# A selective-scan layer laid out as 4 states x 32 channels per tile instead of 128 channels per state

## The chip, the cores and the metric

The program runs on one core of a Trainium2 chip. The metric is the device time of one execution, in microseconds (us). Five engines work side by side, each through its own queue in program order, and meet through semaphores: TensorE (PE; its weight loads are shown as PEld), VectorE (DVE), ScalarE (ACT), GpSimd (POOL), and SyncE (SP), which here only issues DMAs.

## The reference, cut to what matters

For 16 sequences of 1024 rows with 256 columns, a layer of four heads of 128 channels is followed by a quantised feed-forward block. What the change touches is the scan of the first:

```python
xc = conv_b + sum_k xp[:, k:k+L, :] * w[:, k];  x = silu(xc)          # 512 channels = 4 heads x 128
x_dbl = einsum('hod,blhd->blho', xw, xh)                              # per head: dt_r (16), B (16), C (16)
delta = softplus(einsum('hdr,blhr->blhd', dtw, dt_r) + dt_proj_b)     # 128 channels a head
A = -exp(A_log)                                                       # channels x 16 states
def step(s, inp):                                                     # s: channels x states
    s = s * exp(d_t[..., None] * A) + (d_t * u_t)[..., None] * B_t[:, :, None, :]
    y_t = einsum('bhdn,bhn->bhd', s, C_t)
y = (y + x * Dskip) * silu(z);  out = y @ out_proj_w.T
```

Then `x = x + out`, a layer norm, and `fp4(h) @ fp4(w_down)` with `h = silu(gate) * up`, where `fp4` rounds blocks of 16 values to a grid.

## The kernel before, in words

A **unit** is one head over 512 steps of one sequence: 128 units in all. Its scan is 16 **steps** (slots n = 0 to 15), one a state, each over 128 partitions (the channels) x 512 time steps. For step g, PE spreads row g of B over all partitions into one of three PSUM banks (`spread_b`, L939), DVE multiplies it with delta x u (L878, one slot ahead of its scan), ACT makes the decay `exp(delta * A)` (L445, three slots ahead, in a ring of four), and DVE scans (L888). POOL multiplies each pair of scanned states with two rows of C (`weigh`, L619), which a DMA has laid on all 128 partitions (`spread_c`, L375, 512 KB a pair, 8 a unit); for every other pair POOL also adds the two products (L623); PE adds them up in `ybank` with products with the identity (`sum_up`, L951), 12 a unit. DVE takes `ybank` into `yg` (L749).

Everything else is work by due slots, laid into the same 16 slots of each unit by `timetable`: a job's slot s stands in the program at n = s mod 16, one unit later for each 16. "pre" jobs prepare unit u+2 and u+1: input projection, convolution, silu, the product that gives dt, B and C, a split into bf16 pieces (`hi`, `less`, `mid`, `pieces`), and the softplus, for which ACT changes its table to the logarithm and back (L555, L436). "norm" jobs load and normalise the rows of the units ahead, and "post" jobs run the second norm and the feed-forward block for one tile of 128 rows a unit: among them, at n = 2, PE's two products for the gate (L1044), at n = 3, ACT's tanh of it (`sg`, L473) and PE's products with `wu` (L1011), and at n = 4, DVE's `silu_gate` (L812), which stands before the scan of that slot.

What sets the order: each engine's queue is this program, slot by slot. Inside a slot the order is that of the code. In PE's slot: spread, sum, then the side jobs in the order in which `side` lists them. In ACT's slot before: `xnt` (norm 19), the logarithm (pre 25), the decay, then norm and post jobs, and the pre jobs with `hi` (pre 15), `mid` (pre 17) and `pieces` (pre 19) at the end. In DVE's slot: the product for the next step, the jobs of `between`, the scan, the jobs of `behind`. The carry of a sequence's first half is copied by DVE after the 16th scan of the unit (L893, 64 units). The kernel's loop runs over 14 trips of 8 units; what is ahead and behind is written out. Ahead of the first unit, SP loads the constants (`constants`, L343), weights are quantised by DVE and POOL, and ACT waits for all constants before `aneg` (L573).

The bank `bank_c` is shared in time by z's projection, the softplus and the rounding of the feed-forward block.

Of the kernel before, what the change touches and what calls it, by code (L numbers as in the profile page):

```python
# [17 lines left out]
F32 = mybir.dt.float32  # L18
# [34 lines left out]

DB_BANKS = 3
# [4 lines left out]


PAIRS = NST // 2
C_RING = 4
P_RING = 4


ADDED = (0, 2, 4, 6)
# [49 lines left out]
def build(nc, hidden, win_t, conv_w, conv_b, xw, dtw, dt_b, a_log, dskip, wo_t, w_gate, w_up, w_down,  # L116
# [4 lines left out]
    with ExitStack() as ctx:  # L121
# [11 lines left out]
        sel = sb("sel", [NST, P], BF16)  # L133
# [7 lines left out]
        dtws = sb("dtws", [HEADS, P])  # L141
# [9 lines left out]
        state = sb("state", [NST, CH])  # L151
        carry = sb("carry", [HEADS, NST])
        decay = sb("decay", [RING, CH])
        cs = sb("cs", [C_RING, 2, CH])
        prod = sb("prod", [P_RING, 2, CH])
        delta = sb("delta", [2, CH])
        du = sb("du", [2, CH])
        uu = sb("uu", [4, CH])
        sz = sb("sz", [4, CH])
        pieces = sb("pieces", [2, CH], BF16)  # L160
# [6 lines left out]
        tz = sb("tz", [CH])  # L167
        xdbl = sb("xdbl", [CH])
# [49 lines left out]

        b_spread = sem("b_spread")
        c_written = sem("c_written")  # L220
        c_landed = [sem(f"c_landed{i}") for i in range(C_RING)]
# [4 lines left out]
        added = sem("added")  # L226
# [14 lines left out]
        xd_mm = sem("xd_mm")  # L241
        xd_evac = sem("xd_evac")
        res_mm = sem("res_mm")
        mid_done = sem("mid_done")
        pieces_done = sem("pieces_done")
# [40 lines left out]
        c_rows = nc.dram_tensor("c_rows", (2, NST, CH), F32, kind="Internal").ap()  # L286

# [4 lines left out]
        stage = [state[:, 4 * i:4 * i + 4, :].rearrange("p a b -> p (a b)") for i in range(4)]  # L292
# [10 lines left out]
        QUANT_POOL = {44: (0, 3), 56: (1, 3), 68: (2, 3), 88: (0, 9), 108: (1, 9), 126: (2, 9)}  # L303

# [36 lines left out]
        def _(sp):  # L341
# [3 lines left out]
            def constants(j):  # L345

                if j != -7:
                    return
                const(less[:, :, :], less_c)
                const(win[:, :, :], win_t.rearrange("(k p) n -> p k n", p=P))  # L350
                const(cw[:, :, :], conv_w)
                const(cb[:, :], conv_b)
                const(xws[:, :, :], xw)
                const(dtws[:, :, :], dtw)
                const(dtb[:, :], dt_b)
                const(alog[:, :, :], a_log)
                const(dsk[:, :], dskip)
                const(sel[:, :, :], sel_c[:, 0:NST, :])
                const(wo[:, :, :], wo_t.rearrange("(h p) n -> p h n", p=P))
# [3 lines left out]
            free_reg = sp.alloc_register("free_count")  # L363
            rows_reg = sp.alloc_register("rows_count")

            def spread_c(b, u, p):

                slot = p % C_RING
                free = held(sp, free_reg, u.val(PAIRS, p + 1 - C_RING))
                if p == 0:  # L370
                    rows_in = held(sp, rows_reg, u.val(16, 16))
                    wait(sp, c_written, rows_in)
                wait(sp, weighted, free)
                rows = c_rows[u.mod(2), 2 * p:2 * p + 2, :].rearrange("n c -> (n c)")
                sp.dma_start(cs[:, slot, :, :].rearrange("p n c -> p (n c)"),  # L375
                             rows.unsqueeze(0).broadcast_to([P, 2 * CH])).then_inc(c_landed[slot], 16)

            def step(b, j, n):
# [4 lines left out]
                if n % 2:  # L383
                    p = (n + 5) // 2
                    w = u + p // PAIRS
                    if w.within(UNITS):
                        spread_c(b, w, p % PAIRS)
# [24 lines left out]
        CONSTS = 11 * 16  # L412
# [3 lines left out]
        def _(act):  # L416
# [7 lines left out]
            def step(b, j, n):  # L424
# [8 lines left out]
                if v := due("pre", 25):  # L433
# [4 lines left out]
                for ahead in () if due("pre", 24) else (2, 3) if due("pre", 25) else (3,):  # L438
                    g = Ix(b, j * NST + n + ahead, TRIP)
                    if g.within(STEPS):  # L440
                        gu, gn = g.k // NST, g.k % NST
                        if gn == 0:
                            wait(act, sp_pool, Ix(b, gu, PER).val(3, 2))
                        wait(act, scanned, g.val(plus=1 - RING))
                        act.activation(decay[:, g.k % RING, :], delta[:, gu % 2, :], ACT.Exp,  # L445
                                       scale=aneg[:, gu % HEADS, gn:gn + 1]).then_inc(decayed, 1)

# [34 lines left out]
                if t := due("post", 24):  # L482
                    wait(act, v_norm, t.val(plus=1))
                    wait(act, h_round, (t + -2).val(4, 4))
                    if isinstance(b, int):
                        wait(act, sz_done, t.val(plus=7) if (t + 7).within(UNITS) else UNITS)
# [43 lines left out]
                if v := due("pre", 15):  # L530
                    wait(act, xd_mm, v.val(plus=1))
                    wait(act, dt_mm, v.val())
                    wait(act, res_mm, v.val(2))
                    wait(act, c_written, v.val(16))
                    act.activation(hi[:, :], pbank[:, :], ACT.Copy).then_inc(xd_evac, 1)  # L535
                    act.activation(xdbl[:, :], pbank[:, :], ACT.Copy).then_inc(xd_evac, 1)
                if v := due("pre", 17):
                    wait(act, res_mm, v.val(2, 1))
                    act.activation(mid[:, :], pbank[:, :], ACT.Copy).then_inc(mid_done, 1)
                if v := due("pre", 19):  # L540
                    wait(act, res_mm, v.val(2, 2))
                    wait(act, b_spread, v.val(NST, -NST))
                    act.activation(pieces[:, v.mod(2), :], pbank[:, :], ACT.Copy).then_inc(pieces_done, 1)
                if v := due("pre", 21):
# [6 lines left out]
                if v := due("pre", 22):  # L551
                    wait(act, dt_evac, v.val(2, 1))
                    act.activation(spe[:, :], spe[:, :], ACT.Exp, scale=-1.0).then_inc(sp_act, 1)
                if v := due("pre", 23):
                    act.preload_act_table_set("natural_log")  # L555
                if v := due("pre", 26):
                    wait(act, v_round, (u + -5).val(2, 2))
                    if isinstance(b, int):
                        wait(act, h_round, (u + -7).val(4, 4))
# [7 lines left out]
            def place_weight(j):  # L567
# [3 lines left out]
                if j == -4:  # L571
                    act.wait_ge(ld_const, CONSTS)
                    act.activation(aneg[:, :, :], alog[:, :, :], ACT.Exp).then_inc(a_exp, 1)  # L573
                if j == -3:
                    act.wait_ge(a_ready, 5)
# [19 lines left out]
        def _(pool):  # L595
# [17 lines left out]
            def weigh(w, p):  # L613

                c, r = p % C_RING, p % P_RING
                wait(pool, scanned, w.val(NST, 2 * p + 2))
                wait(pool, c_landed[c], w.val(16 * PAIRS // C_RING, 16 * (p // C_RING + 1)))
                wait(pool, summed, w.val(PAIRS, p + 1 - P_RING))
                pool.tensor_tensor(prod[:, r, :, :], state[:, 2 * p:2 * p + 2, :], cs[:, c, :, :],  # L619
                                   ALU.mult).then_inc(weighted, 1)  # L620
                if p in ADDED:
                    wait(pool, weighted, w.val(PAIRS, p + 1))
                    pool.tensor_tensor(prod[:, r, 0, :], prod[:, r, 0, :], prod[:, r, 1, :],  # L623
                                       ALU.add).then_inc(added, 1)

            def step(b, j, n):
# [13 lines left out]
                if w := due("scan", 20):  # L640
# [4 lines left out]
                if v := due("pre", 26):  # L645
# [3 lines left out]
                if v := due("pre", 27):  # L649
                    wait(pool, sp_corr, v.val(plus=1))  # L650
                    wait(pool, sp_pool, v.val(3, 1))
                    wait(pool, decayed, v.val(NST, -NST))
                    pool.tensor_tensor(delta[:, v.mod(2), :], spl[:, :], spe[:, :], ALU.subtract).then_inc(sp_pool, 1)
                if v := due("pre", 28):
# [536 lines left out]
```

## Time and profile before

| | us |
|---|---|
| median of 3 runs | 5382.28 (5376.45 to 5386.91) |
| profiled execution | 5384.97 |
| its span in the trace | 5382.9 |

| engine | busy, share of the span |
|---|---|
| DVE | 96% |
| POOL | 82% |
| PE | 77% |
| ACT | 61% |

The first line of the page gives the span; then come each engine's busy time, the same in 40 slices, the DMA queues, and the groups of instructions, each with its line, what it writes and reads, how often it ran, its busy time, the mean duration of one, and the idle time just before them with what ended it. The timeline lists instructions of one engine in order of time, with the idle time ahead in brackets. Start times there are us from the span's start.

### The profile page before, as it was taken

The page shows a single profiled execution, that of the slowest core. Times are in us where ns is not written, and L with a number is a line of the kernel's source. Part 1 is how long each engine was busy: PE and PEld are TensorE (multiplying, and loading weights), DVE is VectorE, ACT ScalarE, POOL GpSimd, SP SyncE. Part 2 cuts the span into 40 slices and gives each one's busy share as a digit, 9 for nine tenths or more (in the row PEclk, how much of TensorE's full clock was granted, in tenths as well). Part 3 has the DMA queues.
Part 4 walks back from the last instruction along what each step waited for, and adds up shares of the span by engine and source line. Part 5 has one row for each costly group of instructions (what it writes and reads, how often), then busy time and mean ns, then how long its engine had stood idle before and what let it go on. Part 6 is the DMA issues. An engine that isn't in the chain of part 4 may idle for free.

```text
span 5382.9 us, 77607 instructions
## 1 busy us (share of the span) xinstructions
PE 4155.3 (77%) x12609; PEld 2142.2 (40%) x12844; DVE 5186.5 (96%) x7901; ACT 3306.0 (61%) x5776; POOL 4395.8 (82%) x3089
## 2 busy tenths in 40 slices
PE   4678777777777777777777777777777777777778
PEld 1234434444443444434344344443444434344444
DVE  6999999999999999999999999999999999999997
ACT  4666666666666666666666666666666666666663
POOL 5888888888888888888888888888888888888885
PEclk8999999999999999999999999999999999999999
DMA  2333333333333333333333333333333333333331
GB/s 93 134 116 115 114 112 112 115 115 115 109 116 111 116 114 114 115 112 115 113 113 111 115 112 114 111 118 112 112 114 113 116 110 117 112 112 114 114 113 45
DMA packets 211343, 602.12 MB, mean 112 GB/s; under 512 B 25446, under 2 KB 76774, under 8 KB 210790
## 3 DMA queue, kind: packets, MB, share of 16 engines
q1 hardware_dynamic: 209088, 594.30, 32.9%
q14 instruction: 415, 3.40, 0.2%
q8 instruction: 138, 2.26, 0.2%
q10 hardware_dynamic: 1702, 2.16, 0.2%
HBM read 575.39 MB, written 20.97 MB: 111 GB/s over the span
## 4 chain that ended last, share of the span: by engine, by line
DVE 42%; issue 20%; PE 16%; ACT 7%; POOL 6%; DVEq 3%; ACTq 1%; POOLq 0%; another core or an unknown queue 0%
DVE state L888 18%; DVE db L878 8%; PE ybank L951 7%; ACT decay L445 4%; DVE pbank L827 3%; DVEq L100 3%; PE bank_c L961 2%; POOL prod L619 2%; DVE hh L812 2%; DVE hw L803 2%; PE db L939 2%; PE bank_a L1058 1%; DVE hs L698 1%; DVE hh L820 1%; ACT sg L473 1%
## 5 line engine op out<-in xcount | busy, mean ns | idle before, releaser
L619 POOL TENSOR_TENSOR prod<-state,cs 128x1024 f32<-128x1024 f32 x1024 | 2415.3, 2359 | 799.2 <-DVE state L888 759.5
L445 ACT ACTIVATE decay<-delta,aneg 128x512 f32<-128x512 f32 x2048 | 1449.7, 720 | 1342.7 <-DVE state L888 1305.4
L951 PE MATMUL ybank<-prod,ident 128*128 128x512 f32 x3072 | 1568.4, 621 | 95.7 <-DVE state L888 89.5
L939 PE MATMUL db<-pieces,sel 128*128 128x512 bf16 x1844 | 719.5, 391 | 1015.9 <-DVE state L888 982.3
L878 DVE TENSOR_TENSOR db<-db,du 128x512 f32<-128x512 f32 x2048 | 1414.3, 691 | 69.4 <-issue 37.9
L888 DVE TENSOR_TENSOR_SCAN state<-decay,carry,db 128x512 f32<-128x512 f32 x1024 | 1297.4, 1267 | 0.0
L888 DVE TENSOR_TENSOR_SCAN state<-decay,db 128x512 f32<-128x512 f32 x1024 | 1234.9, 1206 | 0.0
L939 PEld LDWEIGHTS db<-pieces,sel 128*128 128x128 bf16 x2048 | 200.4, 98 | 1722.3 <-DVE state L888 1587.4
L951 PEld LDWEIGHTS ybank<-prod,ident 128*128 128x128 f32 x3072 | 564.8, 194 | 317.5 <-issue 264.0
L623 POOL TENSOR_TENSOR prod<-prod 128x512 f32<-128x512 f32 x512 | 650.0, 1270 | 40.1
L1058 PE MATMUL bank_a<-wd,ht 128*128 128x256 f32 x1536 | 446.1, 404 | 17.7 <-DVE state L888 15.7
L1058 PEld LDWEIGHTS bank_a<-wd,ht 128*128 128x128 f32 x1536 | 322.0, 210 | 200.0 <-issue 166.7
L1044 PE MATMUL bank_a<-wg,vt 128*128 128x352 f32 x1024 | 352.0, 467 | 15.6 <-DVE state L888 10.5
L1011 PE MATMUL bank_b<-wu,vt 128*128 128x352 f32 x1024 | 344.7, 459 | 0.7
L961 PE MATMUL bank_c<-xnt,win 128*128 128x512 f32 x512 | 328.2, 730 | 5.5 <-DVE spe L774 4.7
L961 PE MATMUL pbank<-xnt,win 128*128 128x512 f32 x512 | 264.9, 600 | 2.1 <-ACT spr L550 1.4
L1081 PE MATMUL bank_a<-wo,yg 128*128 128x256 f32 x1024 | 262.3, 379 | 2.0 <-DVE ot L840 1.1
L1011 PEld LDWEIGHTS bank_b<-wu,vt 128*128 128x128 f32 x1024 | 194.6, 190 | 142.5 <-issue 82.2
L1081 PEld LDWEIGHTS bank_a<-wo,yg 128*128 128x128 f32 x1024 | 194.2, 190 | 116.2 <-issue 99.3
L1044 PEld LDWEIGHTS bank_a<-wg,vt 128*128 128x128 f32 x1024 | 186.5, 196 | 73.2 <-issue 9.8
L535 ACT ACTIVATE hi<-pbank 128x512 bf16<-128x512 f32 x128 | 76.4, 597 | 204.8 <-PE pbank L1087 204.8
L430 ACT ACTIVATE xnt<-bank_b 128x256 f32<-128x256 f32 x128 | 49.1, 383 | 242.4 <-PE bank_b L1000 242.4
(125 smaller groups left out, 6436.3 us busy)
## 6 DMA issues: line engine op xcount, KB each, us to landing
cs<-c_rows SPq DMA_DIRECT2D x1024, 512.0 KB, 3.6
xin<-in_hidden SPq DMA_DIRECT2D x128, 128.0 KB, 3.8
xres<-in_hidden SPq DMA_DIRECT2D x128, 128.0 KB, 3.1
out_x<-ot SPq DMA_DIRECT2D x128, 128.0 KB, 3.6
c_rows<-xdbl SPq DMA_DIRECT2D x128, 32.0 KB, 3.6
win<-in_win_t SPq DMA_DIRECT2D x1, 1024.0 KB, 10.3
state<-in_w_gate ACTq DMA_DIRECT2D x1, 704.0 KB
state<-in_w_up ACTq DMA_DIRECT2D x1, 704.0 KB
```

The source lines that it names most:

```text
L445: act.activation(decay[:, g.k % RING, :], delta[:, gu % 2, :], ACT.Exp, scale=aneg[:, gu % HEADS, gn:gn + 1]).then_inc(decayed, 1)
L619: pool.tensor_tensor(prod[:, r, :, :], state[:, 2 * p:2 * p + 2, :], cs[:, c, :, :], ALU.mult).then_inc(weighted, 1)
L623: pool.tensor_tensor(prod[:, r, 0, :], prod[:, r, 0, :], prod[:, r, 1, :], ALU.add).then_inc(added, 1)
L878: dve.tensor_tensor(t[:, :], t[:, :], du[:, gu % 2, :], ALU.mult).then_inc(db_done, 1)
L888: dve.tensor_tensor_scan(state[:, n, :], decay[:, n % RING, :], db[DB_BANK[g.k % TRIP]][:, :], start, ALU.mult, ALU.add).then_inc(scanned, 1)
L939: pe.matmul(db[DB_BANK[g.k % TRIP]][:, :], sel[:, gn, :], pieces[:, gu % 2, :], start=True, stop=True).then_inc(b_spread, 1)
L951: last = pe.matmul(ybank[:, :], ident[:, :], prod[:, p % P_RING, k, :], start=(p == 0), stop=(p == PAIRS - 1 and k == 1))
L961: return pe.matmul((pbank, bank_c)[part][:, :], win[:, k, part * DI + h * P:part * DI + (h + 1) * P], xnt[:, v.mod(8) // 4, k, :], start=( ...
L1011: last = pe.matmul(bank_b[:, 0:HALF], vt[:, k, :], wu[:, k, part * HALF:(part + 1) * HALF], start=(k == 0), stop=(k == KM - 1))
L1044: last = pe.matmul(bank_a[:, 0:HALF], vt[:, k, :], wg[:, k, part * HALF:(part + 1) * HALF], start=(k == 0), stop=(k == KM - 1))
L1058: last = pe.matmul(bank_a[:, 0:DM], ht[:, k, :], wd[:, k, :], start=(k == 0), stop=(k == KI - 1))
L1081: last = pe.matmul(bank_a[:, 0:DM], yg[:, t.mod(8) // 4, h, i * P:(i + 1) * P], wo[:, h, :], start=(h == 0), stop=(h == HEADS - 1))
```

## The change

A tile's 128 partitions now hold 4 states of 32 channels instead of one state of 128 channels (partition p holds channel p // 4 and state p mod 4 of the block). A unit still has 16 steps: step n is states 4(n // 4) to 4(n // 4)+3 of channels 32(n mod 4) to 32(n mod 4)+31.

- delta and delta x u of a unit are written to DRAM (`dd_rows`, 512 KB, pre 23) and read back as four tiles `bc` with each channel on four partitions (512 KB each, pre 25 and 26). Rows of C come as four tiles `crow` of 256 KB. That is 3 MB a unit in broadcasts, where it was 4 MB. One weight matrix `selb` spreads four rows of B at once.
- `weigh` keeps its 8 products of 128x1024 a unit, and POOL's adds are gone. `sum_up` is now called at n = 2, 6, 10 and 14, with four products of 32 columns (`place`), each into its own 32 partitions of `ybank`: 16 a unit.
- The state ring is 8 slots, not 16. The carry is copied by ACT, 4 states at a time, at n = 1, 5, 9, 13. `yg` moves from n = 3 to n = 4 (scan 19 to 20) on DVE, and its product with sz on POOL from scan 20 to 22.
- Of pre: delta no longer waits for the x_dbl rows. A product of both weights (`wdt`) is made once, and gives dt from u at slot 14; the softplus follows at 15 to 22, six slots earlier; hi, mid and pieces stand two slots later and at the start of ACT's slot, with the less products at the end of PE's.
- Constants: `a_log` is loaded in 64 DMAs of 128 elements, `sel` comes ahead of `win`; two more constants are made by DVE (READY is 7).

```diff
@@ sync @@
                 const(less[:, :, :], less_c)
+                const(sel, sel_c[:, 0:NST, :])
                 const(win[:, :, :], win_t.rearrange("(k p) n -> p k n", p=P))
...
-                const(alog[:, :, :], a_log)
+                for h in range(HEADS):
+                    for i in range(NST):
+                        k, c = i // PART * PART, i % PART * WIDE
+                        sp.dma_start(alog[:, h, i:i + 1], a_log[c:c + WIDE, h, k:k + PART],
+                                     allow_slow_non_contiguous=True).then_inc(ld_const, 16)
...
+            def spread_rows(w, i):
+                rows = dd_rows[w.mod(2), i * WIDE:(i + 1) * WIDE, :, :].rearrange("c k t -> c (k t)")
+                sp.dma_start(bc[:, w.mod(2), i, :, :].rearrange("p k t -> p (k t)"),
+                             rows.unsqueeze(1).broadcast_to([WIDE, PART, 2 * CH])).then_inc(bc_landed[i], 16)
...
+                if v := due("pre", 23):
+                    wait(sp, sp_pool, v.val(3, 3))
+                    sp.dma_start(dd_rows[v.mod(2), :, :, :], dd[:, :, :]).then_inc(dd_written, 16)
@@ scalar @@
-                if v := due("pre", 25):
+                if v := due("pre", 17):
+                    wait(act, xd_mm, v.val(plus=1))
...
+                    act.activation(hi[:, :], pbank[:, :], ACT.Copy).then_inc(xd_evac, 1)
+                    act.activation(xdbl[:, :], pbank[:, :], ACT.Copy).then_inc(xd_evac, 1)
+                if v := due("pre", 19):
+                    wait(act, res_mm, v.val(2, 1))
+                    act.activation(mid[:, :], pbank[:, :], ACT.Copy).then_inc(mid_done, 1)
...
+                if v := due("pre", 19):
                     wait(act, sp_act, v.val(3, 1))
                     act.activation(spl[:, :], spe[:, :], ACT.Ln, bias=1.0).then_inc(sp_act, 1)
                     act.preload_act_table_set("exp_and_others")
-                for ahead in () if due("pre", 24) else (2, 3) if due("pre", 25) else (3,):
+                for ahead in () if due("pre", 18) else (2, 3) if due("pre", 19) else (3,):
...
+                if n % 4 == 1:
...
+                        act.activation(carry[:, w.mod(HEADS), 4 * k:4 * k + 4],
+                                       state[:, 4 * k % S_RING:4 * k % S_RING + 4, CH - 1], ACT.Copy).then_inc(carried, 1)
@@ gpsimd @@
-                if p in ADDED:
-                    wait(pool, weighted, w.val(PAIRS, p + 1))
-                    pool.tensor_tensor(prod[:, r, 0, :], prod[:, r, 0, :], prod[:, r, 1, :],
-                                       ALU.add).then_inc(added, 1)
@@ vector @@
-                if w := due("scan", 19):
-                    wait(dve, summed, w.val(PAIRS, PAIRS))
+                if w := due("scan", 20):
+                    wait(dve, summed, w.val(BLOCKS, BLOCKS))
...
-                if n == NST - 1 and g.within(STEPS) and not late:
-                    wait(dve, scanned, g.val(plus=1))
-                    dve.tensor_copy(carry[:, h, :], state[:, :, CH - 1]).then_inc(carried, 1)
-                    wait(dve, carried, u.div(PER, HEADS, h + 1))
@@ tensor @@
+                wait(pe, weighted, w.val(PAIRS, 2 * q + 2))
+                for i in range(4):
+                    s = (4 * q + i) % (2 * P_RING)
+                    last = pe.matmul(ybank[32 * i:32 * i + 32, :], place[:, :], prod[:, s // 2, s % 2, :],
+                                     start=(q == 0), stop=(q == BLOCKS - 1))
                 last.then_inc(summed, 1)
...
                 if v := due("pre", 14):
                     wait(pe, u_done, v.val(plus=1))
+                    pe.matmul(pbank[:, :], wdt[:, v.mod(HEADS), :], uu[:, v.mod(4), :],
+                              start=True, stop=True).then_inc(dt_mm, 1)
+                if v := due("pre", 16):
+                    wait(pe, dt_evac, v.val(2, 2))
                     pe.matmul(pbank[:, :], xws[:, v.mod(HEADS), :], uu[:, v.mod(4), :],
                               start=True, stop=True).then_inc(xd_mm, 1)
+                if v := due("pre", 18):
+                    wait(pe, xd_evac, v.val(2, 2))
+                    pe.matmul(pbank[:, :], less[:, 0, :], hi[:, :], start=False, stop=True,
+                              skip_group_check=True).then_inc(res_mm, 1)
```

## Rows read from the trace of the kernel before

**Rows 1.** Busy time of the engines: us from:to, length, then each engine, clock, DMA.
```profile
2000.00:3000.00 1000.00, 779.68 (x2381) 403.89 (x2426) 975.29 (x1493) 623.70 (x1092) 828.60 (x584) 0.96 0.33 113
```
**Rows 2.** Groups of instructions, whole run, on DVE, PE and POOL.
```profile
L619 POOL TENSOR_TENSOR prod<-state,cs 128x1024 f32<-128x1024 f32 x1024 | 2415.3, 2359 | 799.2 <-DVE state L888 759.5
L951 PE MATMUL ybank<-prod,ident 128*128 128x512 f32 x3072 | 1568.4, 621 | 95.7 <-DVE state L888 89.5
...
L878 DVE TENSOR_TENSOR db<-db,du 128x512 f32<-128x512 f32 x2048 | 1414.3, 691 | 69.4 <-issue 37.9
...
L888 DVE TENSOR_TENSOR_SCAN state<-decay,db 128x512 f32<-128x512 f32 x1024 | 1234.9, 1206 | 0.0
...
L623 POOL TENSOR_TENSOR prod<-prod 128x512 f32<-128x512 f32 x512 | 650.0, 1270 | 40.1
```
**Rows 3.** What DVE waited for, whole run: us in total, times, longest.
```profile
DVE db L878 <- issue: 37.9, 13, 3.1
DVE yg L749 <- PE ybank L951: 24.5, 29, 3.9
```
**Rows 4.** DVE's timeline around one copy of the carry.
```profile
2056.28 1.21 DVE L888 TENSOR_TENSOR_SCAN state<-decay,db 128x512 f32<-128x512 f32 x1
2057.52 0.95 DVE L893 COPY carry<-state 128x16 f32<-128x16 f32 x1
2058.62 0.70 DVE L878 TENSOR_TENSOR db<-db,du 128x512 f32<-128x512 f32 x1
```
**Rows 5.** PE's timeline, slot n = 2 of one unit.
```profile
2022.83 0.39 PE L939 MATMUL db<-pieces,sel 128*128 128x512 bf16 x1 [1.47 <-DVE state L888]
2023.06 1.88 PE L951 MATMUL ybank<-prod,ident 128*128 128x512 f32 x4
2024.78 0.38 PE L985 MATMUL pbank<-mid,less 128*128 128x512 bf16 x1
2024.99 0.38 PE L1000 MATMUL bank_b<-ident,xn 128*128 128x128 f32 x2
2025.21 1.35 PE L1044 MATMUL bank_a<-wg,vt 128*128 128x352 f32 x4
2026.39 0.38 PE L939 MATMUL db<-pieces,sel 128*128 128x512 bf16 x1
```
**Rows 6.** ACT's timeline: the gate's tanh, then the logarithm and its table.
```profile
2026.30 0.50 ACT L465 ACTIVATE v<-x,mv 128x256 f32<-128x256 f32 x1
2026.70 0.45 ACT L473 ACTIVATE sg<-bank_a 128x352 f32<-128x352 f32 x1
2027.04 0.59 ACT L543 ACTIVATE pieces<-pbank 128x512 bf16<-128x512 f32 x1
...
2039.48 0.62 ACT L435 ACTIVATE spl<-spe 128x512 f32<-128x512 f32 x1
2040.12 1.28 ACT L436 ACT_TABLE_LOAD   x1
2041.41 1.95 ACT L445 ACTIVATE decay<-delta,aneg 128x512 f32<-128x512 f32 x3
2043.27 0.58 ACT L561 ACTIVATE bank_c<-spe 128x512 f32<-128x512 f32 x1
```
**Rows 7.** DVE's timeline, slot n = 4 of the same unit.
```profile
2028.11 0.69 DVE L878 TENSOR_TENSOR db<-db,du 128x512 f32<-128x512 f32 x1
2028.70 0.51 DVE L812 SCALAR_TENSOR_TENSOR hh<-sg,bank_a 128x352 f32<-128x352 f32 x1
```
**Rows 8.** Start of the run: the DMA queue of SP, a norm's statistics on DVE.
```profile
6.68 0.53 SPq L343 DMA_DIRECT2D alog<-in_a_log  x1
...
29.06 0.41 DVE L758 BATCH_NORM_STATS2 stats<-xin 128x6 f32<-128x256 f32 x1
```
**Rows 9.** DMA issues: what, how often, KB each, median us to landing.
```profile
cs<-c_rows SPq DMA_DIRECT2D x1024, 512.0 KB, 3.6
```
**Rows 10.** PE's timeline where its granted clock fell to half after a gap.
```profile
2089.27 0.61 PE L939 MATMUL db<-pieces,sel 128*128 128x512 bf16 x1 [2.06 <-DVE state L888]
```

More of the change, by code:

```diff
@@ L52 @@
 RING = 4
+PAIRS = NST // 2
+PART = 4
+BLOCKS = NST // PART
+WIDE = P // PART
+P_RING = 4
+S_RING = 8
+S_PAIRS = S_RING // 2
 DB_BANKS = 3
@@ L132, in build @@
         ident = sb("ident", [P])
-        sel = sb("sel", [NST, P], BF16)
+        place = sb("place", [WIDE])
+        selb = sb("selb", [BLOCKS, P], BF16)
         less = sb("less", [2, P], BF16)
@@ L167, in build @@
         tz = sb("tz", [CH])
+        pieces = sb("pieces", [2, CH], BF16)
         xdbl = sb("xdbl", [CH])
@@ L483, in step @@
                     wait(act, v_norm, t.val(plus=1))
-                    wait(act, h_round, (t + -2).val(4, 4))
-                    if isinstance(b, int):
-                        wait(act, sz_done, t.val(plus=7) if (t + 7).within(UNITS) else UNITS)
+                    if not isinstance(b, int):
+                        wait(act, sp_corr, t.val(plus=7))
+                    else:
+                        wait(act, sp_corr, min(t.val(plus=7), UNITS))
+                        wait(act, sz_done, min(t.val(plus=7), UNITS))
+                        wait(act, h_round, (t + -2).val(4, 4))
                     act.activation(bank_c[:, 0:DM], v2[:, :], ACT.Abs, scale=POWER).then_inc(v_abs, 1)
@@ L530, in step @@
                 if v := due("pre", 15):
[L531 to L544, printed above, removed]
                     h = v.mod(HEADS)
@@ L965, in side @@
                     wait(pe, xnt_done, v.div(4, 4, 4))
-                    wait(pe, dt_evac, v.val(2))
+                    wait(pe, pieces_done, v.val())
+                    if peeled and v.val() == 0:
+                        pe.wait_ge(w_kept, 2)
                     in_proj(v, 0, 0)
@@ L1098, in turn_weight @@
                     pe.wait_ge(ld_const, CONSTS)
-                    pe.wait_ge(a_ready, 5)
+                    for h in range(HEADS):
+                        last = pe.transpose(pbank[:, h * P:(h + 1) * P], xws[:, h, :], ident[:, :])
+                    last.then_inc(w_turned, 1)
+                    pe.wait_ge(w_kept, 1)
+                    for h in range(HEADS):
+                        last = pe.matmul(bank_c[:, h * P:(h + 1) * P], xwt[:, h, :], dtws[:, h, :],
+                                         start=True, stop=True)
+                    last.then_inc(w_turned, 1)
+                    pe.wait_ge(a_ready, READY)
                 if w is None:
```

210 lines of the change are left out of this document (118 added, 92 removed).

## The prediction

> **What bounds the kernel now.** The window table comes first: over 1000 us of the steady part DVE is busy for 975 us, POOL for 829, PE for 780, ACT for 624 [rows 1]. DVE is the bound, so a change pays only by what it takes from DVE's queue or from DVE's waits, and costs whatever it makes DVE wait. Next the groups of instructions: DVE's product takes 691 ns and its scan 1206 ns on average [rows 2], sixteen of each a unit, and their means are those of every single row that I looked at, whether POOL or a DMA was busy beside them or not. So these rows hold no lengthening by a shared resource that an idler POOL could give back. Then DVE's waits: the largest is 37.9 us in 13 pieces without a releaser, up to 3.1 us each, which is the loop's edge, and 24.5 us before `yg`, for the last sums of PE [rows 3]. The large costs that the change cuts thus lie where there is slack: POOL's 512 adds are 650 us of POOL's time [rows 2], and the DMA of C lands 3.6 us after its issue [rows 9], several slots before it is read. Neither is worth anything by itself.
>
> **What leaves DVE.** The 64 copies of the carry. Around one of them the scan starts at 2056.28 and the next product at 2058.62, 2.34 us; a scan followed directly by a product takes 1.12 of it, so the copy costs 1.2 us here, of which its record is 0.95 [rows 4]. This was a long one; I take 0.9, with 0.7 and 1.2 as bounds: 64 x 0.9 = 57 us (45 to 77). On ACT the copies of 4 columns cost some 0.15 us each beside DVE's scans, at slots where the states have been scanned already; nothing for DVE. Products, scans and the rest of DVE's queue keep shape and number. The wait before `yg` goes, as `yg` stands one slot later: 24 us. The loop's edge stays. Together 5382.9 - 57 - 24 = 5302.
>
> **Start of the run.** SP issues a constant's DMA in about 0.53 us, `a_log` among them [rows 8]. It now issues 64 where it issued one: 63 x 0.53 = 33 us, ahead of the third `xin` on the same queue. Those rows were used by DVE at 29.06 [rows 8]; issued after some 44 us they come at about 46, and DVE's quantising steps are queued behind that norm: 17 us late. PE's two weight products, the new DVE constants and the DRAM round trip before the first decay add to the start, while delta, which no longer waits for hi, mid and pieces, comes earlier; I set these against each other. The bounds are 0 (all regained) and 33. I take 17: 5302 + 17 = 5319 us. This is what the change would give with no new wait.
>
> **The new wait.** I followed each slot of the changed program through the queues of PE, ACT and DVE with the durations of one unit. One place doesn't close, slots 2 to 4. Before, PE in slot 2 does the spread, the sum, the less product, the transposes and the gate's products, and ACT takes the gate's tanh in slot 3 at 2026.70 [rows 5, 6]. It ends at 2027.15; DVE uses it at 2028.70 [rows 7], so there are 1.55 us of slack. Now the first less product stands behind the gate's, and ACT's slot 3 begins with a wait for it, then mid, the logarithm, a table load, two decays and the norm's centring, and the tanh only after these. Step by step, with S for the time that PE needs for its group of sums: the group starts at 2023.06; transposes take 0.22 (2024.99 to 2025.21) and the gate 1.18 (2025.21 to 2026.39) [rows 5], so the less product starts at 2024.46 + S, lasts 0.38, and ACT starts mid at 2024.9 + S. Mid, like pieces, takes 0.5 without its overlap; logarithm to table load 0.64, table load 1.29, two of the three decays 1.24, centring 0.40, tanh 0.45 [rows 6]: 4.5 us. The gate is ready at 2029.4 + S. DVE would want it at 2028.70 still, since `yg` moves from slot 3 to just before it and nothing else changes between slot 1 and there. DVE waits S + 0.7 us in every unit. Who queues behind DVE's wait: scan 4, and with it the spread of slot 5, decay 8, POOL's second product. Nothing gives it back, as DVE had nothing else to wait for.
>
> **How large is S?** Before, the last pair of the unit took PE 1.72 us in four records: a product is two records of 0.43 us [rows 5], and 12 products are the 24 x 128 = 3072 records of the group [rows 2]. Now the group of slot 2 has four products of the same 512 columns, eight records. If they run one after another, S = 3.44. If all four run beside each other, as they use 32 columns and 32 partitions each, S = 0.86. Nothing in this trace shows a product of 32 columns, so both are open. I take the middle: the two records of one product use the same columns, so only the second record of one can lie beside the first of the next, in program order: 5 x 0.43 = 2.15. To this I add 0.2 for letting the pipe run empty at the changes of shape, from nothing up to twice the 0.17 us by which a record of 0.39 outlasts its share of the queue [rows 5]. The wait is then 2.35 + 0.7 = 3.05 us, and 128 x 3.05 = 390. The sum: 5319 + 390 = 5709 us of span. The profiled execution took 2 us more than its span and 3 more than the median, so this is also the median's forecast, rounded to 5710.
>
> Two rules of the Trainium skill bear on S, and no run here shows either yet. The page TensorEngine Tiling (Array Packing), section Key Properties, says that different tiles can load weights and multiply in parallel, which read alone is the rival with S = 0.86. The same list says that changing the tiling mode drains TensorE, which speaks against eight switches a unit.
>
> The other slots hold. The next largest group is at slot 6: with S = 2.15 the spread for step 9 is done some 3.9 us after scan 5, and DVE asks after 4.1; with S = 3.44 it is late by 0.9, and so is the spread at slot 15 behind the group of slot 14. The tiles of delta are ready in time: POOL ends delta x u about 5.5 us after scan 5, a write and a broadcast of 512 KB at 3.6 us or more each [rows 9] end by 16 us, and DVE's first product of the next unit comes after 21. SP's wait for delta x u holds back `spread_c` of the same slot, which is needed four slots later.
>
> **Rivals.** (1) All four sums together: S = 1.06 with the change of shape, a wait of 1.8 us, 5319 + 128 x 1.8 = 5549. For it speaks that the four write different partitions; against it that a product has two records. (2) The sums one after another: S = 3.64, a wait of 4.35, 5319 + 557 = 5876; with the late spreads of slots 8 and 0, another 1.8, 6106. For it speaks that every pair of sums in the trace is serial; against it that those use the whole width. (3) The clock: PE idles for about 4 us during the new wait, and a spread after a gap of 2.06 us took 0.61 us where it takes 0.39, the granted clock being at its lower level, 1.2 GHz [rows 10]. If this comes in each unit just behind the gap, PE's slots 5 and 6 take twice as long, the spread for step 9 is late by 1 to 2 us, and the time is 5710 + 128 x 1.2 = 5860. (4) The other side, faster: ACT's chain fits in. It decides at the point where tanh ends within 5.9 us of scan 1, which would need the table load and the logarithm to be over before the less product lands; by the order of ACT's queue they can't be, unless I misread that order or what the wait asks for. The time would be 5319, 1.2% faster, from the copies of the carry alone. (5) The change doesn't do what it says, in that POOL's and the DMAs' relief is not seen in the time: that is part of all of these.
>
> **How the numbers follow.** Likeliest, 5710 with its own range of 5640 to 5800: 0.42. Rival 1, 5500 to 5640: 0.2. Rival 2: 0.2. Rival 3: 0.06. Rival 4: 0.1. Something else within 0.2% of before or between: 0.02. The range of 5520 to 6110 leaves out rival 4 and the tails of 1 and 2. A measurement of this kernel can tell about 0.2% from no change; faster by more 0.1, within it 0.02, slower 0.88.
>
> **What would show it.** DVE's waits in the changed kernel should have one large row, `silu_gate` waiting for ACT's sg, about 128 times and near 3 us; ACT should wait before mid for PE's less product. The records of the group of four sums give S directly. POOL's busy share should fall to about 65% and change nothing. The first norm delayed by constants should show DVE idle between 30 and 46 us. The prediction is wrong if DVE's waits show no such row, or a row of like size on another wait, such as a spread late at slot 8 or bc tiles that land after DVE wants them.

## The result and the profile after

| | median, us | ratio to the kernel before (95% interval) |
|---|---|---|
| before | 5379.4 (5374.3 to 5386.9, 4 runs) | |
| changed kernel | 5677.5 (5664.3 to 5682.3, 4 runs) | 1.0549 (1.0527 to 1.0572) |

The change makes the kernel 5.5% slower. The forecast was 5710, and the place it named is the place. The profiled execution has a span of 5680.4 us, 297.5 more than before. First the page's busy times and groups, to be held against [rows 2] and the table of before:

```profile
PE 3922.1 (69%) x13880; PEld 1730.9 (30%) x13880; DVE 5170.3 (91%) x7839; ACT 3346.1 (59%) x6034; POOL 3738.7 (66%) x2577
...
L671 POOL TENSOR_TENSOR prod<-state,crow 128x1024 f32<-128x1024 f32 x1024 | 2414.0, 2358 | 1207.1 <-DVE state L934 1200.2
...
L1003 PE MATMUL ybank<-prod,place 128*32 128x512 f32 x4096 | 670.2, 732 | 25.1 <-POOL prod L671 21.7
...
L857 DVE SCALAR_TENSOR_TENSOR hh<-sg,bank_a 128x352 f32<-128x352 f32 x256 | 129.4, 506 | 296.2 <-ACT sg L526 296.2
```

POOL lost its 650 us of adds and only idles longer, by its waits for DVE's scans (1200 us, before 760). DVE's busy share fell from 96% to 91% though its busy time hardly changed (5170 for 5187): it waits. What it waited for (in total, times, longest; before in [rows 3]):

```profile
DVE hh L857 <- ACT sg L526: 296.2, 128, 3.1
DVE db L944 <- PE db L993: 68.2, 113, 1.9
DVE stats L803 <- DMA xin<-in_hidden: 30.1, 1, 30.1
...
DVE state L934 <- issue: 13.0, 8, 2.2
DVE ot L885 <- PE bank_a L1098: 11.8, 8, 7.0
...
DVE yg L794 <- PE ybank L1003: 1.1, 1, 1.1
```

The first row is the new wait of the forecast, `silu_gate` for the gate's tanh, once in each of the 128 units. Two rows of the same view of the kernel before, for the waits for PE's last products of the block (`ot`) and for the spreads (`db`):

```profile
DVE ot L840 <- PE bank_a L1058: 33.3, 76, 5.3
...
DVE db L878 <- PE db L939: 21.4, 58, 2.2
```

Added up, all rows of this view are 503 us, and 175 before. DVE's busy time is 16 less. 328 - 16 = 312, and the span grew by 297.5. The difference is idle time too short for the view to list, 21 us before and 7 after (span less busy time less waits); most of what went stood around the copies of the carry.

The chain that ended last, in the window of one unit's slots 1 to 4, shows the whole wait (start, length, what):

```profile
2024.74 1.20 DVE state L934
2025.99 0.39 PE db L993
2026.38 1.00 PE ybank L1003 x8
2027.37 0.37 PE bank_b L1040 x2
2027.74 1.19 PE bank_a L1084 x4
2028.93 0.23 PE pbank L1135
...
2030.31 1.28 ACT L483
...
2033.34 0.36 ACT sg L526
```

From the scan of slot 1 it runs over PE's group of sums, the transposes, the gate's products and the less product (L1135), to ACT's logarithm, its table load (L483), the decays, the centring and the tanh. The same on ACT's timeline, to be held against [rows 6], and DVE's row at its end, against [rows 7]:

```profile
2029.18 0.60 ACT L475 ACTIVATE mid<-pbank 128x512 bf16<-128x512 f32 x1 [0.94 <-PE pbank L1135]
2029.67 0.62 ACT L482 ACTIVATE spl<-spe 128x512 f32<-128x512 f32 x1
2030.31 1.28 ACT L483 ACT_TABLE_LOAD   x1
2031.61 1.33 ACT L492 ACTIVATE decay<-bc,aneg 128x512 f32<-128x512 f32 x2
2032.85 0.49 ACT L518 ACTIVATE v<-x,mv 128x256 f32<-128x256 f32 x1
2033.25 0.44 ACT L526 ACTIVATE sg<-bank_a 128x352 f32<-128x352 f32 x1
```
```profile
2033.81 0.52 DVE L857 SCALAR_TENSOR_TENSOR hh<-sg,bank_a 128x352 f32<-128x352 f32 x1 [1.74 <-ACT sg L526]
```

Mid to the end of the tanh is 4.51 us (2029.18 to 2033.69). The wait is 1.74.

**The wait comes in two sizes.** Another unit has 3.06 us. PE's timeline of slot 2, first of the unit with 1.74, then of that with 3.06:

```profile
2025.99 0.39 PE L993 MATMUL db<-pieces,selb 128*128 128x512 bf16 x1 [2.47 <-DVE state L934]
2026.31 1.06 PE L1003 MATMUL ybank<-prod,place 128*32 128x512 f32 x8
2027.30 0.44 PE L1040 MATMUL bank_b<-ident,xn 128*128 128x128 f32 x2
2027.58 1.35 PE L1084 MATMUL bank_a<-wg,vt 128*128 128x352 f32 x4
```
```profile
1505.72 0.61 PE L993 MATMUL db<-pieces,selb 128*128 128x512 bf16 x1 [2.41 <-DVE state L934]
1506.26 1.94 PE L1003 MATMUL ybank<-prod,place 128*32 128x512 f32 x8
1508.13 0.69 PE L1040 MATMUL bank_b<-ident,xn 128*128 128x128 f32 x2
1508.61 1.61 PE L1084 MATMUL bank_a<-wg,vt 128*128 128x352 f32 x4
```

The group of four sums takes 0.99 us (2026.31 to 2027.30) in the one and 1.87 in the other. The granted clock of the second stretch, from the windows (from:to, length, PE busy, clock, DMA share, GB/s):

```profile
1504.00:1508.00 4.00, 2.28 (x9) 0.71 0.43 107
1508.00:1512.00 4.00, 4.00 (x18) 0.86 0.00 0
```

So in some units TensorE's granted clock falls to its lower level (1.2 GHz) at slot 2, behind a gap of 2.4 us; in others it stays at 2.4 GHz behind a gap of the same length. It doesn't always fall ahead of the group: in some units the gate's products are the first at the lower level. Over the whole run 59 of the 128 waits are 2.7 us or longer, 3.01 on average. In 58 of these units the clock was below full between the start of the group of sums and ACT's mid, and in none of the other 69.

### The profile page after: what moved, and what is told of

Read it like the earlier page. It is cut to its first block, busy times and chain, and to the rows that moved or that the text cites. A ratio compares the mean times of both kernels' runs of the same rounds, so it can differ in the third digit from the quotient of the medians.

```text
span 5680.4 us, 79523 instructions
## 1 busy us (share of the span) xinstructions
PE 3922.1 (69%) x13880; PEld 1730.9 (30%) x13880; DVE 5170.3 (91%) x7839; ACT 3346.1 (59%) x6034; POOL 3738.7 (66%) x2577
## 4 chain that ended last, share of the span: by engine, by line
DVE 41%; issue 27%; PE 15%; ACT 8%; DVEq 6%; POOL 2%; SPq 1%; ACTq 0%; DMA 0%; POOLq 0%
DVE state L934 17%; DVE db L944 7%; DVE pbank L872 5%; DVEq L100 5%; PE ybank L1003 4%; PE bank_a L1084 4%; ACT L483 3%; ACT decay L492 2%; PE pbank L1013 2%; PE db L993 2%; DVE hw L848 2%; DVE hs L743 2%; DVE hh L865 1%; POOL prod L671 1%; PE bank_b L1040 1%
## 5 line engine op out<-in xcount | busy, mean ns | idle before, releaser
L671 POOL TENSOR_TENSOR prod<-state,crow 128x1024 f32<-128x1024 f32 x1024 | 2414.0, 2358 | 1207.1 <-DVE state L934 1200.2
L492 ACT ACTIVATE decay<-bc,aneg 128x512 f32<-128x512 f32 x2048 | 1460.3, 719 | 1706.5 <-DVE state L934 1665.1
L993 PE MATMUL db<-pieces,selb 128*128 128x512 bf16 x2048 | 875.3, 428 | 1621.6 <-DVE state L934 1590.7
L944 DVE TENSOR_TENSOR db<-db,bc 128x512 f32<-128x512 f32 x2048 | 1395.0, 681 | 70.0 <-PE db L993 68.2
L993 PEld LDWEIGHTS db<-pieces,selb 128*128 128x128 bf16 x2048 | 204.9, 100 | 2553.0 <-DVE state L934 2426.8
L1003 PE MATMUL ybank<-prod,place 128*32 128x512 f32 x4096 | 670.2, 732 | 25.1 <-POOL prod L671 21.7
L700 POOL TENSOR_TENSOR dd<-spl,spe 128x512 f32<-128x512 f32 x128 | 163.0, 1273 | 577.2 <-DVE spe L819 577.2
L1084 PE MATMUL bank_a<-wg,vt 128*128 128x352 f32 x1024 | 537.2, 667 | 5.0 <-DVE hh L857 3.9
L857 DVE SCALAR_TENSOR_TENSOR hh<-sg,bank_a 128x352 f32<-128x352 f32 x256 | 129.4, 506 | 296.2 <-ACT sg L526 296.2
L717 POOL TENSOR_TENSOR hh<-hh,hs 128x704 f32<-128x704 f32 x128 | 177.6, 1387 | 9.7 <-DVE hh L851 9.7
L712 POOL TENSOR_TENSOR hh<-hh,hs 128x704 f32<-128x704 f32 x128 | 177.5, 1387 | 8.2 <-DVE hs L749 8.2
```

Of the source, the lines that this page charges most:

```text
L492: act.activation(decay[:, g.k % RING, :], bc[:, gu.mod(2), gn % PART, 0, :], ACT.Exp, scale=aneg[:, gu.mod(HEADS), gn:gn + 1]).then_inc(de ...
L671: pool.tensor_tensor(prod[:, r, :, :], state[:, 2 * q:2 * q + 2, :], c, ALU.mult).then_inc(weighted, 1)
L944: dve.tensor_tensor(t[:, :], t[:, :], bc[:, w.mod(2), i % PART, 1, :], ALU.mult).then_inc(db_done, 1)
L993: pe.matmul(db[DB_BANK[g.k % TRIP]][:, :], selb[:, gn // PART, :], pieces[:, gu % 2, :], start=True, stop=True).then_inc(b_spread, 1)
L1003: last = pe.matmul(ybank[32 * i:32 * i + 32, :], place[:, :], prod[:, s // 2, s % 2, :], start=(q == 0), stop=(q == BLOCKS - 1))
L1084: last = pe.matmul(bank_a[:, 0:HALF], vt[:, k, :], wg[:, k, part * HALF:(part + 1) * HALF], start=(k == 0), stop=(k == KM - 1))
```

## The experiments

The changed kernel is the base of the edits unless it is said otherwise. Each ratio is to runs of the kernel before on the same chip. A difference to the changed kernel, in us, is one between chips: the kernel before had a median of 5379 us beside the changed kernel and 5386 to 5388 beside the experiments, so such a difference is good to about 8 us.

**1. Do the four sums run beside each other because they write four quarters?**

```diff
-                    last = pe.matmul(ybank[32 * i:32 * i + 32, :], place[:, :], prod[:, s // 2, s % 2, :],
-                                     start=(q == 0), stop=(q == BLOCKS - 1))
+                    o = 32 * i if q == 0 else 0
+                    last = pe.matmul(ybank[o:o + 32, :], place[:, :], prod[:, s // 2, s % 2, :],
+                                     start=(q == 0), stop=(q == 0 and i > 0) or (q == BLOCKS - 1 and i == 3))
```

> The changed kernel, but the groups of sums of slots 10, 14 and 2 write all four products into the same 32 partitions (the group of slot 6 is unchanged). The sums are not those of the reference then, the work is the same. If products into four different quarters of the partitions run beside each other and those into one quarter can't, the group of slot 2 takes 8 x 0.43 = 3.4 us instead of the 1.0 us of the changed kernel, and the wait of silu_gate for the tanh, S + a constant, grows by 2.4 us a unit from 2.3 to about 4.7, plus up to 1.8 us for late spreads: 5980 to 6200 us. If the short group has another reason (the 32 columns alone), nothing changes: 5680.

Measured: 6195.7 us, ratio 1.1507 (1.1481 to 1.1533). The time is within the expected range. The groups on PE's timeline; the second line is that of slot 6, unchanged:

```profile
2004.61 3.62 PE L1004 MATMUL ybank<-prod,place 128*32 128x512 f32 x8
...
2030.43 1.06 PE L1004 MATMUL ybank<-prod,place 128*32 128x512 f32 x8
...
2039.49 5.32 PE L1004 MATMUL ybank<-prod,place 128*32 128x512 f32 x8 [0.36 <-POOL prod L671]
```

(The last ran in part at the lower clock, at 0.68 on average.) The same eight records take 3.6 us in one quarter and 1.06 in four. The overlap comes from the quarters, not from the 32 columns. Where the time went was a miss in part: the wait for the tanh grew only from 2.3 to 2.9 us a unit, and the late spreads took the rest.

```profile
DVE db L944 <- PE db L993: 493.9, 315, 4.2
DVE hh L857 <- ACT sg L526: 374.5, 128, 3.1
```

**2. The logarithm one slot earlier.**

```diff
-                if v := due("pre", 19):
+                if v := due("pre", 18):
                     wait(act, sp_act, v.val(3, 1))
                     act.activation(spl[:, :], spe[:, :], ACT.Ln, bias=1.0).then_inc(sp_act, 1)
                     act.preload_act_table_set("exp_and_others")
-                for ahead in () if due("pre", 18) else (2, 3) if due("pre", 19) else (3,):
+                for ahead in (3,):
```

> The changed kernel with the logarithm and its table load one slot earlier on ACT (n = 2 instead of 3), so that only one decay and no table load stand between the less product and the gate's tanh. Theory of the chain (ACT's queue holds the tanh back): the chain is 2.5 us shorter, the wait of silu_gate falls from 2.3 us a unit to 0 to 0.3, and the time by 260 to 300 us, to 5380 to 5420. Rival (PE is late: its clock is lower and its products long, and the tanh waits for PE's gate products): the wait stays near 2 us and the time above 5600.

Measured: 5470.7 us, ratio 1.0162 (1.0139 to 1.0185), 207 us less than the changed kernel, where 260 to 300 were expected: a miss. The wait for the tanh is gone (8 us in all), and a new one has come, of about 1 us a unit:

```profile
DVE hw L848 <- ACT bank_c L556: 128.8, 127, 2.4
DVE db L944 <- PE db L993: 44.5, 52, 2.0
```

L556 is the abs for the rounding (post 50), which stands in ACT's slot 2 behind the logarithm; DVE's `step_up` waits for it in slot 3. The theory of the chain holds; that nothing else stood behind the moved work was wrong, and cost 129 us.

**3. Mid at the end of ACT's slot 3,** behind the tanh, so that the logarithm doesn't wait for the less product.

```diff
-                if v := due("pre", 19):
-                    wait(act, res_mm, v.val(2, 1))
-                    act.activation(mid[:, :], pbank[:, :], ACT.Copy).then_inc(mid_done, 1)
...
                     act.activation(bank_c[:, :], spe[:, :], ACT.Identity, bias=1.0).then_inc(sp_act, 1)
+                if v := due("pre", 19):
+                    wait(act, res_mm, v.val(2, 1))
+                    act.activation(mid[:, :], pbank[:, :], ACT.Copy).then_inc(mid_done, 1)
```

> The changed kernel with mid moved to the end of ACT's slot 3, behind the tanh. ACT then no longer waits for the less product before its logarithm. Theory of the chain: the logarithm can start 1.5 us earlier than in the changed kernel (right after xnt), the tanh ends about when DVE asks for it; the wait falls from 2.3 to 0.2 to 0.6 us a unit, 5410 to 5470 us. Rival that PE is late: above 5600.

Measured: 5458.4 us, ratio 1.0138 (1.0116 to 1.0160), as expected; the wait for the tanh is 64 us in all (0.5 a unit). PE's queue was the same, and only ACT's order had changed: the logarithm no longer stands behind a wait for the less product. So it was this order that held the tanh back.

**4. a_log in one DMA,** laid out by the host in the order of the tiles.

```diff
-                for h in range(HEADS):
-                    for i in range(NST):
...
+                const(alog[:, :, :], a_log)
```

> The changed kernel with a_log laid out by the host so that one DMA loads it, as before, instead of 64. Theory: the 64 issues hold up the third xin, and DVE waits 30 us for it once: 5650 us, 0.5% under the changed kernel. Rival: the delay is regained in the start of the run: 5680.

Measured: 5650.1 us, ratio 1.0494 (1.0471 to 1.0517), 27 us less, as expected. The row of 30.1 us is gone from DVE's waits. In the changed kernel SP's queue had held (64 issues in 48 us, 0.75 each):

```profile
7.15 47.99 SPq L370 DMA_DIRECT2D alog<-in_a_log  x64
```

**5. The three together, with the logarithm behind the abs.** Mid and a_log as in 3 and 4; the logarithm with its table load moves to the end of ACT's slot 2 (pre 18, after all other work), and the two decays stay in slot 3.

```diff
-                if v := due("pre", 19):
-                    wait(act, sp_act, v.val(3, 1))
-                    act.activation(spl[:, :], spe[:, :], ACT.Ln, bias=1.0).then_inc(sp_act, 1)
-                    act.preload_act_table_set("exp_and_others")
...
+                if v := due("pre", 18):
+                    wait(act, sp_act, v.val(3, 1))
+                    act.activation(spl[:, :], spe[:, :], ACT.Ln, bias=1.0).then_inc(sp_act, 1)
+                    act.preload_act_table_set("exp_and_others")
```

> The changed kernel with three edits: the logarithm and its table load at the end of ACT's slot 2 (behind the rounding's abs, which the one-slot-earlier version held up by 0.9 us a unit), mid at the end of slot 3, and a_log in one DMA. Theory of the chain: ACT's slot 3 is then two decays, centring and tanh, which ends about 0.8 us before DVE asks for it; neither the wait for the tanh (2.3 us a unit) nor that for the abs is left, only 60 to 80 us of late spreads: 5330 to 5370 us, 0.3 to 1% faster than the kernel before. Rival: a third wait takes their place, 5400 or more.

Measured: 5336.2 us, ratio 0.9912 (0.9896 to 0.9927): within what was expected; the same layout is now faster than the kernel before. No third wait took the place:

```profile
DVE db L940 <- PE db L989: 71.1, 109, 1.7
...
DVE hh L853 <- ACT sg L515: 11.0, 15, 1.9
```

**6. The clock, tried in the wrong gap.** Twelve idle products (nobody reads what they compute) in slot 4, into `ybank` between its reading and the next unit's first sum:

```diff
+                if w := due("scan", 4):
+                    wait(pe, y_taken, w.val())
+                    for _ in range(12):
+                        pe.matmul(ybank[:, :], selb[:, 0, :], pieces[:, w.mod(2), :], start=True, stop=True)
```

> The changed kernel with 12 idle products (bf16, 512 columns, 2.6 us) on PE in slot 4, in the gap of 4.5 us that the wait for the tanh leaves. Theory of the clock: the gap falls to 2 us, the clock rises from 0.87 to 0.95, the waits for the tanh that were 3.1 us become 1.8 like the others, and late spreads go: 80 to 140 us less, 5540 to 5600 us. If the clock has no part: 5680.

Measured: 5699.8 us, ratio 1.0578 (1.0556 to 1.0600), a miss: 5540 to 5600 was expected, and there is no gain and perhaps some loss. The gap behind slot 4 is filled and the mean clock rose from 0.871 to 0.912, but the gap ahead of slot 2 is as it was, and the wait for the tanh is not shorter:

```profile
DVE hh L857 <- ACT sg L526: 324.7, 128, 3.1
DVE db L944 <- PE db L993: 83.3, 110, 2.7
```

Now 88 of the 128 waits are 2.7 us or longer, where it was 59, and in all 88 units the clock was below full in slot 2. Why more units fall there is open.

**7. The clock, in the gap ahead of slot 2.** Eight idle products in slot 1, into `bank_a` between its reading and the gate:

```diff
+                if t := due("post", 33):
+                    if (t + 1).within(TILES):
+                        wait(pe, x1_done, t.val(plus=2))
+                        for _ in range(8):
+                            pe.matmul(bank_a[:, :], selb[:, 0, :], pieces[:, u.mod(2), :], start=True, stop=True)
```

> The changed kernel with 8 idle products (bf16, 512 columns, 1.7 us) on PE in slot 1, in the gap of 2.4 us ahead of slot 2, instead of those in slot 4. Theory: the waits for the tanh are 1.74 us where slot 2 runs at TensorE's higher clock and 3.06 where the clock has fallen before it (group of sums 1.9 us instead of 1.0); with the gap ahead of slot 2 filled, nearly all are 1.74: 296 us in all become 225 to 240, and the time 5610 to 5640 us. If the clock isn't the reason for the 3.06: 5680.

Measured: 5580.9 us, ratio 1.0357 (1.0337 to 1.0376): 97 us less than the changed kernel, for PE work that computes nothing, and more than expected. The idle products and the spread behind them, then DVE's waits:

```profile
2033.66 1.90 PE L1129 MATMUL bank_a<-pieces,selb 128*128 128x512 bf16 x8
2036.20 0.39 PE L993 MATMUL db<-pieces,selb 128*128 128x512 bf16 x1 [0.65 <-DVE state L934]
```
```profile
DVE hh L857 <- ACT sg L526: 224.8, 132, 3.0
DVE db L944 <- PE db L993: 52.4, 68, 1.9
```

The wait for the tanh falls by 71 us and is 1.7 us on average; late spreads fall by 16. The clock from the group of sums to mid was full in all units, and one wait is 2.7 us or longer, where it was 59. The mean clock over the run, 0.881, is lower than in experiment 6. What counts is the clock in slot 2, not its mean. The page TensorE: Matmul & The Clock Gate of the Trainium skill (Part 1) says that the default is throttled and activity releases it; the two fillers agree with it, and show that it pays only where the chain runs.

**8. The same two fillers on the kernel of experiment 5.** With eight products in slot 4:

> As ln_end_alog, with 8 idle products (bf16, 512 columns, 1.7 us in all) on PE in slot 4 of every unit, into the bank of sums after it is read and before the next unit's first sum. Theory of the clock (late spreads come from TensorE at its lower clock after a gap): the granted clock rises from 0.90 to 0.95 or more, DVE's waits for spreads halve, 20 to 40 us faster than ln_end_alog. Rival (spreads are late because PE has too much queued): the products make them later, 0 to 60 us slower.

Measured: 5323.9 us, ratio 0.9892 (0.9873 to 0.9911), 12 us less than experiment 5, with intervals that overlap, and the waits for spreads fell from 71 to 56 us. The granted clock was 0.920 for 0.914. The expected direction, but too little to call. With eight products in slot 1:

> ln_end_alog with the same 8 idle products in slot 1. With the wait for the tanh gone a slow slot 2 costs little: 5310 to 5340 us, within 0.3% of ln_end_alog. If slot 2 still sets DVE's waits at the lower clock: 30 us faster or more.

Measured: 5311.1 us, ratio 0.9857 (0.9839 to 0.9876), the fastest kernel of this study; waits for spreads are 46 us. It is 25 us less than experiment 5, 0.5%, and the intervals don't overlap. That is within the time expected but not within the 0.3%, and a little under the 30 us of the rival: at the lower clock slot 2 still cost something, through late spreads.

**9. The copy of the carry alone,** in the kernel before: DVE's copy goes, ACT copies four states at n = 1, 5, 9 and 13, and DVE waits for them before it scans over them (the lines of these waits are left out).

```diff
...
-                    dve.tensor_copy(carry[:, h, :], state[:, :, CH - 1]).then_inc(carried, 1)
...
+                if n % 4 == 1:
+                    w = u if n > 1 else u + -1
+                    k = (n - 5) // 4 % 4
+                    if w.within(UNITS) and w.mod(PER) < HEADS:
+                        wait(act, scanned, w.val(NST, 4 * k + 4))
+                        act.activation(carry[:, w.mod(HEADS), 4 * k:4 * k + 4],
+                                       state[:, 4 * k:4 * k + 4, CH - 1], ACT.Copy).then_inc(carried, 1)
```

> The kernel before with the carry copied by ACT, four states at a time, as in the change, and nothing else. Theory: the 64 copies cost DVE 0.9 us each, 45 to 77 us in all: 5310 to 5340 us, a ratio near 0.989. Rival: DVE gets the time back as waits for PE, ratio 0.997 to 1.

Measured: 5317.6 us, ratio 0.9877 (0.9859 to 0.9896), as expected: 70 us, or 1.1 a copy. DVE's busy time fell by 52 us, and its waits for `yg`, 24.5 us before, to 7; its waits for spreads rose by 12 (21.4 to 33.4):

```profile
DVE yg L756 <- PE ybank L960: 6.7, 4, 4.5
```

This one small part of the change gives 1.2% without the new layout. The new layout, with its order mended and idle products added, gives 1.4%, and the intervals of the two overlap. Without idle products it gives 0.9% (experiment 5), though it too has the copies on ACT: beside the same runs of the kernel before it is 18 us slower than this edit alone, with no run of one as fast as any of the other. So no gain is left to the layout itself.

## Why the prediction was right, point by point

- **The bound.** DVE, and only its queue and its waits counted. POOL's 650 us and a megabyte less of broadcasts a unit gave nothing that can be seen: DVE's busy time fell by 16, which is the copies (52, by experiment 9) less a longer scale (36, below).
- **The new wait.** Right in place, in number (128) and in working: the constant part of the wait, all but S, was 0.7 and is 1.74 - 0.99 = 0.75. Experiments 2 and 3 move one piece of the chain each, experiment 5 both, and the wait goes. That the tanh waits for ACT's order is shown.
- **S.** This term was mis-sized. I took 2.35 us, the last record of one product beside the first of the next, plus a change of shape. It is 0.99 at the higher clock: all four beside each other, as in rival 1. The step that failed is the argument that a product's two records must fall one after another in program order and hold back the next product; experiment 1 shows that they do hold each other back within one quarter and not over four. With the rule of the Trainium skill, page TensorEngine Tiling (Array Packing), section Key Properties, that tiles multiply in parallel, the trace agrees (0.99 us for four, where one alone is 0.86). The 0.2 for the change of shape was near. The group starts 0.32 us after the spread ahead of it, where the sums of before started 0.23 after [rows 5] (medians over the run 0.320 and 0.226). From its last record to the next product are 0.52 us, and from the last of the sums before to the next were 0.43, medians too. That is 0.09 us at each change, 0.19 a group.
- **The clock.** It was rival 3, set behind the gap in slots 5 and 6. It is real but sits in slot 2 as well: 59 of the 128 units, at some 3.0 us instead of 1.74. The wait is 296 us in all instead of 390. At the full clock it would be 128 x 1.74 = 223, and experiment 7 measured 225. So at the full clock the forecast wait was 167 us too long, and the lower clock put back 73 of it.
- **Late spreads.** I said that the other slots hold. DVE's waits for spreads went from 21 to 68 us. Behind the gap of 4.5 us the gate's second half, the group of slot 6 and the projection run at the lower clock, as rival 3 had it (1.93 us for a group at 2039.57).
- **The start.** 17 us, measured 27 by experiment 4. An issue took 0.75 us in the row of 64, not 0.53 as the single one; DVE waited 30 us, and hardly any of it was regained.
- **The copies.** 57 for the copies and 24 for `yg` were 81; alone in the kernel before they are 70. The copies were 52 us of busy time and some 10 in short gaps, `yg` 18, and 12 came back as waits for spreads, which I had left out.
- **A lengthening that I had not looked for.** I had looked at the products and scans. DVE's scale of the norm's blocks took 159 ns on average over the whole run before and 440 after: 36 us in 128. More below.

So 390 + 17 - 81 = 326 was expected and 298 measured. The wait for the tanh was 94 too much; late spreads (47), the scale (36) and the start (10 to 13) were not counted or too small, and together they make up for it. Of the 28 us that are left, 8 are the copies and `yg` (52 + 14 in short gaps + 23 = 89 instead of 81). The rest lies in waits that I had said would stay: the idle time without a releaser fell from 38 to 13 us and the waits before `ot` from 33 to 12, while small waits rose by some 30 together. The near hit is luck in part: the errors cancel. The mechanism was right, and the likeliest size of S was not.

## What to carry to other kernels

Moving work to other slots is costed by what stands behind it in its new place: write down each queue in order, from the event that releases its first piece to the one for which the bound engine waits. A logarithm, its table load and a copy that waits for PE, all ahead of a tanh, cost 5% here; with the first two at the end of the slot before and the copy behind the tanh, the wait was 11 us in all instead of 296. And try the parts of a large change one by one: the smallest, a copy taken off the bound engine, held nearly all of the gain, and the layout itself none.

## What the runs showed of the hardware

**Products of 32 columns into four quarters of one PSUM bank run beside each other, fp32 too:** four of 512 columns in 0.99 us, and into one quarter in 3.6. Each change between such products and those of the full width cost 0.09 us.

**Idle products in a gap ahead of a chain that the bound engine waits for can pay:** the same kernel with 1.7 us of them in the gap of 2.4 us ahead of slot 2 was 97 us faster, though PE did more. The clock in slot 2 was then full in all units, where it had fallen in 58. Twelve such products in another gap gave nothing.

**A short VectorE operation beside one of GpSimd can end only when that one does.** In the changed kernel the scale of 16 elements (L746) falls where POOL computes delta, which now stands six slots earlier:

```profile
2038.03 1.26 POOL L700 TENSOR_TENSOR dd<-spl,spe 128x512 f32<-128x512 f32 x1 [3.89 <-DVE spe L819]
2038.89 0.44 DVE L746 TENSOR_SCALAR vs<-vs 128x16 f32<-128x16 f32 x1
```

Its group in the steady part, and that of the kernel before:

```profile
L746 DVE TENSOR_SCALAR vs<-vs 128x16 f32<-128x16 f32 x69 | 32.3, 468 | 0.0
```
```profile
L701 DVE TENSOR_SCALAR vs<-vs 128x16 f32<-128x16 f32 x72 | 11.4, 158 | 0.0
```

Over the whole run 122 of the 128 scales run beside this operation. They take 0.26 to 0.50 us, and every one ends 0.03 us after POOL's operation does; the other six take 0.18 or less. In the kernel before, the single copies of the carry show the same, 16 elements too. The copy of [rows 4], which took 0.95 us, ends at 2058.47, and this ended at 2058.44:

```profile
2057.06 1.38 POOL L667 TENSOR_TENSOR hh<-hh,hs 128x704 f32<-128x704 f32 x1
```

So do 60 of the 64 copies (0.32 to 0.96 us); the four beside POOL's adds took 0.18. The mean of all is 0.70, so about 0.5 us of a copy's record may have been a wait for POOL, which moving POOL's operation might have saved too; no run tried that.

DVE's products and scans show no such thing. The page SBUF — State Buffer of the Trainium skill (section Who interferes with whom) says that only one pair of ports is shared between the two engines, as an exclusive lock; operations that all end 0.03 us after POOL's agree with it. No run here moved POOL's operation alone, so the cause is argued from the end times, not shown by an experiment.
